# Stacks of queries and keys loaded by 5 DMAs with a repeated source in place of 13

## The reference

```python
q, k, v = jnp.split(x @ Wi.T + bi, 3, axis=-1)      # each to [B, H=16, T, HD=8]
scores = jnp.einsum('bhqd,bhkd->bhqk', q, k) / math.sqrt(HD)
scores = scores + mask[None]                        # causal, with ALiBi slopes
attn = jax.nn.softmax(scores, axis=-1)
out = jnp.einsum('bhqk,bhkd->bhqd', attn, v)
```

## Time and profile before

| | |
|---|---|
| median of 3 runs | 3465.85 us (3462.48 to 3480.17) |
| the profiled execution, its time | 3471.59 us |
| its span | 3469.4 us |
| PE busy | 2722.4 us (78%) |
| DVE busy | 1924.7 us (55%) |
| ACT busy | 1436.0 us (41%) |
| POOL busy | 478.3 us (14%) |
| DMA queue of SP | 95.62 MB, 12.6% of 16 engines' span |

### The profile page before, as it was taken

The page is one execution under the profiler, slowest core; times in us unless marked ns, Lnnn a source line. Parts: engine busy times, 40 slices in busy tenths (PEclk is TensorE's granted clock), DMA queues, the critical chain, the costliest instruction groups (busy, mean ns, idle before and its releaser), DMA issues. The chain is left out here.

```text
span 3469.4 us, 38736 instructions
## 1 busy us (share of the span) xinstructions
PE 2722.4 (78%) x12937; PEld 1118.8 (32%) x12937; DVE 1924.7 (55%) x3965; ACT 1436.0 (41%) x2856; POOL 478.3 (14%) x388
## 2 busy tenths in 40 slices
PE   6799876998869988699887689795266679599857
PEld 3233332332413333233343234342022234133225
DVE  4677236772357723677235562436899833677343
ACT  3266332663426643266434303234233243166510
POOL 1000010000100000100005500000688700100000
PEclk8699986999859998699987899897588889699977
DMA  3221012210132100321000000000000001312010
GB/s 82 47 42 30 13 45 48 44 31 13 29 64 45 31 13 14 79 41 34 13 17 1 6 1 0 22 1 12 0 0 0 0 24 36 80 31 44 14 74 13
DMA packets 57180, 98.20 MB, mean 28 GB/s; under 512 B 14438, under 2 KB 30310, under 8 KB 54502
## 3 DMA queue, kind: packets, MB, share of 16 engines
q1 hardware_dynamic: 56972, 95.62, 12.6%
HBM read 77.80 MB, written 16.78 MB: 27 GB/s over the span
## 5 line engine op out<-in xcount | busy, mean ns | idle before, releaser
L619 DVE CUSTOM_DVE_ANT_0 sb_masked_scores<-ps,sb_mask_row 128x128 f32<-128x128 f32 (+7 forms) x1280 | 912.7, 755 | 381.8 <-PE ps L548 375.1
L669 ACT ACTIVATE sb_prob<-ps 128x512 f32<-128x512 f32 (+3 forms) x1920 | 824.0, 495 | 428.5 <-PE ps L566 310.7
L548 PE MATMUL ps<-sb_k_stack,sb_q_stack 78*128 78x512 bf16 (+3 forms) x1920 | 555.8, 366 | 211.7 <-DMA sb_q_stack<-alibi 107.9
L563 PE MATMUL ps<-sb_q_stack,sb_k_stack 81*128 81x512 bf16 (+3 forms) x1920 | 573.4, 339 | 19.3 <-ACT sb_prob L669 2.6
L580 PE MATMUL ps<-sb_prob,sb_v_and_one 128*9 128x512 f32 (+3 forms) x3840 | 407.2, 498 | 2.1 <-ACT sb_o_raw L649 2.1
L563 PEld LDWEIGHTS ps<-sb_q_stack,sb_k_stack 81*128 81x128 bf16 x1920 | 184.2, 99 | 466.9 <-ACT sb_prob L669 311.1
L548 PEld LDWEIGHTS ps<-sb_k_stack,sb_q_stack 78*128 78x128 bf16 x1920 | 164.5, 102 | 445.6 <-DVE sb_row_max L619 230.0
L566 PE MATMUL ps<-sb_mask_kq,sb_ident_bf 128*128 128x128 bf16 x1280 | 267.6, 226 | 0.0
L1827 POOL TENSOR_TENSOR sb_inflow<-sb_delta_u,sb_b_spread 128x1024 f32<-128x1024 f32 x64 | 233.3, 3669 | 45.6 <-ACT sb_b_spread L1810 45.5
L1837 DVE TENSOR_TENSOR_SCAN sb_states<-sb_decay,sb_inflow 128x1024 f32<-128x1024 f32 x64 | 211.4, 3305 | 10.8 <-ACT sb_decay L1816 9.6
L258 ACT ACTIVATE sb_ln_squares<-sb_ln_centred 128x512 f32<-128x512 f32 x68 | 42.8, 629 | 373.9 <-DVE sb_ln_centred L224 373.8
(11 more groups left out here) (353 smaller groups left out, 3518.5 us busy)
## 6 DMA issues: line engine op xcount, KB each, us to landing
sb_k_stack<-k_parts SPq DMA_DIRECT2D x360, 64.0 KB
sb_q_stack<-q_parts SPq DMA_DIRECT2D x120, 192.0 KB
q_parts<-sb_qk_parts SPq DMA_DIRECT2D x80, 96.0 KB, 1.9
k_parts<-sb_qk_parts SPq DMA_DIRECT2D x80, 96.0 KB, 2.0
sb_unpick_sums<-unpick_sums SPq DMA_DIRECT2D x5, 1024.0 KB, 4.9
sb_l_weights<-l_weights SPq DMA_DIRECT2D x4, 1030.0 KB, 5.5
sb_l_gate_and_value<-l_up SPq DMA_DIRECT2D x1, 4096.0 KB, 12.8
sb_xpos<-xpos SPq DMA_DIRECT2D x1, 2048.0 KB
```

What stands on the lines that cost most here:

```text
L548: mm = pe.matmul(M.ps[:, bank + lo // CH, 0:hi - lo], A.qst[0:S1_ROWS, s, j, i * P:(i + 1) * P], A.kst[0:S1_ROWS, s, j, lo:hi], start=True ...
L563: mm = pe.matmul(out[:, a:CH], A.kst[0:S2_ROWS, s, j, kb * P:(kb + 1) * P], A.qst[0:S2_ROWS, s, j, half * CH + a:(half + 1) * CH], start=T ...
L619: dve.tensor_tensor_reduce(out=junk[:, done % 2, 0:w], in0=M.ps[:, bank:bank + 2, :].rearrange("p a q -> p (a q)")[:, 0:w], in1=M.mask_row ...
L669: act.activation(prob[:, st % PROB_STEPS, j, a:CH], M.ps[:, S2_BANK + v % S2_BANKS, a:CH], ACT.Exp).then_inc(exp_done, 1)
```

## The change

The queries' 72 rows are now written by one DMA. Its source is the 96 rows of the group in HBM, each of 1024 tokens, with a leading dimension of size 3 and step 0, so that the same rows are read three times. The keys' rows of one part (24 rows) are likewise written by one DMA, whose source is 32 rows of HBM repeated three times. That makes 3 DMAs for the keys, 1 for the queries and 1 for the bias. Nothing else differs: the same bytes land in the same places, and the waits and their order are as before.

```diff
-STACK_DMAS = 13
+STACK_DMAS = 5
...
 def load_q_stack(eng, A, q_aux, b, g, s, sem):
 
     tok = slice(b * T, (b + 1) * T)
+    rows = A.q_dram[g, :, tok]
+    eng.dma_start(A.qst[0:PAIR_ROWS, s, :, :],
+                  rows.unsqueeze(0).to_broadcast([3, 3 * DH * GROUP, T])).then_inc(sem, 16)
+    eng.dma_start(A.qst[PAIR_ROWS:S1_ROWS, s, :, :], q_aux[g]).then_inc(sem, 16)
+
+
+def load_k_stack(eng, A, b, g, s, sem):
+
+    tok = slice(b * T, (b + 1) * T)
     for k_part in range(3):
         at = 3 * DH * k_part
-        eng.dma_start(A.qst[at:at + 3 * DH, s, :, :],
-                      A.q_dram[g, :, tok].rearrange("(sd j) t -> sd j t", j=GROUP)).then_inc(sem, 16)
-    eng.dma_start(A.qst[PAIR_ROWS:S1_ROWS, s, :, :], q_aux[g]).then_inc(sem, 16)
-
-
-def load_k_stack(eng, A, b, g, s, sem):
-
-    tok = slice(b * T, (b + 1) * T)
-    for k_part in range(3):
-        part = A.k_dram[g, 4 * DH * k_part:4 * DH * (k_part + 1), tok].rearrange("(d j) t -> d j t", j=GROUP)
-        for q_part in range(3):
-            at = (3 * k_part + q_part) * DH
-            eng.dma_start(A.kst[at:at + DH, s, :, :], part).then_inc(sem, 16)
+        rows = A.k_dram[g, 4 * DH * k_part:4 * DH * (k_part + 1), tok]
+        eng.dma_start(A.kst[at:at + 3 * DH, s, :, :],
+                      rows.unsqueeze(0).to_broadcast([3, DH * GROUP, T])).then_inc(sem, 16)
```

More of the change, by code:

```diff
@@ L297, in load_q_stack @@
     tok = slice(b * T, (b + 1) * T)
-    for k_part in range(3):
-        at = 3 * DH * k_part
-        eng.dma_start(A.qst[at:at + 3 * DH, s, :, :],
-                      A.q_dram[g, :, tok].rearrange("(sd j) t -> sd j t", j=GROUP)).then_inc(sem, 16)
+    rows = A.q_dram[g, :, tok]
+    eng.dma_start(A.qst[0:PAIR_ROWS, s, :, :],
+                  rows.unsqueeze(0).to_broadcast([3, 3 * DH * GROUP, T])).then_inc(sem, 16)
     eng.dma_start(A.qst[PAIR_ROWS:S1_ROWS, s, :, :], q_aux[g]).then_inc(sem, 16)
@@ L308, in load_k_stack @@
     for k_part in range(3):
-        part = A.k_dram[g, 4 * DH * k_part:4 * DH * (k_part + 1), tok].rearrange("(d j) t -> d j t", j=GROUP)
-        for q_part in range(3):
-            at = (3 * k_part + q_part) * DH
-            eng.dma_start(A.kst[at:at + DH, s, :, :], part).then_inc(sem, 16)
+        at = 3 * DH * k_part
+        rows = A.k_dram[g, 4 * DH * k_part:4 * DH * (k_part + 1), tok]
+        eng.dma_start(A.kst[at:at + 3 * DH, s, :, :],
+                      rows.unsqueeze(0).to_broadcast([3, DH * GROUP, T])).then_inc(sem, 16)
 def qkv(nc, M, A, W, cols, scale, tables=None):
```

## The result

The changed kernel takes 3560.64 us (median of 4 runs, 3543.14 to 3566.77), the kernel before, run beside it, 3473.01 us. The ratio is 1.0247, with a 95% interval of 1.0213 to 1.0282: slower by 2.5%, some 88 us. Forecast were 63 us more, 3529 us, within 3475 to 3721. The profiled execution took 3561.09 us with a span of 3558.9 us, 89.5 us longer than the span before.

The account below looks back on a forecast made before the run. PE was taken to wait for stack loads at call starts, with loads between groups hidden until their deadline. Starts 24, maxima 9 and between groups 30 us sum to 63 us: 3529 us on the median, range 3475 to 3721.

Parts of the forecast that it names:

- Three engines: Stack loads: the source's outermost size 3 confines each DMA to three engines, busy share near 0.19, some 69 GB/s.
- One load: A stack's load, from first issue to PE: 20.0 us, of which 17.1 us at 69 GB/s.
- The starts: Start of each call: PE begins 4.8 us later, 24 us over five calls.
- Issue: SP's queue: fewer DMAs save about 5.5 us of issuing a load, worth nothing between groups.
- The copies of the maxima: Group 0 of each call: copies queue behind stacks 1 and 2, first `second` 1.8 us late, 9 us in all.
- Between groups: Loads inside calls: 20.0 us against a deadline of 18.37, 1.2 us lost per load, 30 us over five calls.
- Elsewhere: Outside the starts, the copies of the maxima and the loads between groups: the forecast's sum had no term.
- Spread over 12 engines: Rival for stack loads: DMAs spread by destination rows, loads of 11.2 to 11.8 us, about 3447 us; chance 0.08.
- Hidden between groups: Rival: three engines near 26.5 GB/s, loads in time between groups, +13 us at the starts, 3479 us; chance 0.10.
- Much slower for the pace of the engines: Rival for stack loads: three engines at only 14 to 18 GB/s each, 3721 to 3961 us; chance 0.22 (under 19).

Follow-up runs that it names:

- the version with other dimensions outermost: Five DMAs with 8 KB pieces, changed to 24 rows outermost for queries, 8 for keys without repeat, rows reordered: 3438.49 us, 0.9914 to the kernel before.
- FIRST_AHEAD 8: The changed kernel with FIRST_AHEAD, how far `first` runs ahead, at 8 in place of 10: 3492.29 us, 1.0059 to the kernel before.
- 8 KB pieces: The changed kernel's five DMAs, parts stored in HBM by sequence so a row's four heads form one 8 KB piece: 3497.62 us, 1.0098 to the kernel before.
- the queries alone: The kernel before with only the queries' three DMAs made one with a repeated source, the keys by nine as before: 3509.44 us, ratio 1.0133.

## Why the prediction was right, and where its sum was off

*Three engines.* Right: a busy share of 0.18 to 0.22 during loads, and 0.73 to 0.82 in the version with other dimensions outermost. The Trainium skill's rule on a leading zero-stride broadcast (DMA: Bandwidth & Descriptors, Rules for kernel authors) holds here for 3 copies. Its remedy is to put a dimension outermost whose size is a multiple of 16; the run with 24 and 8 outermost, 11.8 us a load, points the same way, but no load of a stack had a multiple of 16 there.

*One load, 20.0 us.* Measured 19.1 to 20.0. The pace was 69 to 81 GB/s for an assumed 69; the packets came a little later, at 1.6 to 2 us for 1.3.

*The starts, 24 us.* Measured 22.6. *Issue, 5.5 us less SP time, worth nothing:* right between groups; where the engines stay, five DMAs have a start 2.5 us shorter than 13.

*The copies of the maxima, 9 us.* Measured 0. The copies did stand behind stacks 1 and 2, as forecast, and in the first call the last landed 5.7 us after its issue. But a pace of some 75 GB/s, for 69, drained these stacks 51.5 us into the first call, for a forecast 53.5, and the last copy came 0.2 to 1.1 us ahead of its need. With FIRST_AHEAD 8, where the copies are wanted earlier, they were late by up to 1.4 us. The mechanism is there, its margin was mis-sized.

*Between groups, 30 us.* This term was mis-sized: 82 us. The waits were nearly as forecast, 25 us in 25 loads, 1.0 us each on average. What the sum left out is what comes behind them: 4 us of idle gaps and 53 us of granted clock at 0.50. The prediction named the clock at its end as what would make the loss larger, and priced it at nothing.

*Elsewhere, 0.* The profiled executions differ by 15.5 us in favour of the changed kernel outside the calls; in the stretch shown above it goes with the granted clock. 22.6 + 0 + 82.4 - 15.5 = 89.5 us. So the forecast of 63 came near partly by luck: two things that it didn't have, +57 and -15, and one that it had too much, 9, partly cancel. The time lies in the range because the range was stretched upwards for slower engines, and they were not slower.

*The rivals.* Spread over 12 engines, 3447 us: not what this change does, but near what its sibling does, with 3438 us; 11.8 us a load is as priced, though there the keys had 8 outermost and the pieces were longer. Hidden between groups, 3479: near it are the runs with FIRST_AHEAD 8 (3492) and with 8 KB pieces (3498). Much slower for the pace of the engines: no, three engines in this pattern run at some 24 GB/s each, the nine of the keys' loads before at 9. Pieces of 8 KB in the 13 DMAs changed nothing in the time (0.9992); why the crowded ones are so slow is open.

## What to carry to other kernels

Look at what stands outermost on both sides of a DMA before you merge small ones: the fewer DMAs here ran on 3 engines in place of 8 and 12. With pieces of 8 KB this cost 1.0%, and with other dimensions outermost the same count of DMAs gained 0.9%. Measure the slack of a prefetch from its issue to its use (18.4 us here, for a load of 15), since the loss rises steeply once it is used up: loads of 19.5 us cost 88 us, loads of 18.6 us cost 31. And price a stall of PE with the clock that it has afterwards: here 1 us of waiting cost 3.3 us on average. It cost 0.15 us over the wait itself where the clock kept 1.00, and 4.7 us over it where the clock stayed low for 10 us.

## What the runs showed of the hardware that was not expected

Waits of about a microsecond are enough for the granted clock to fall to 0.50, in 21 of 25 cases of the changed kernel, some 2 us behind the wait and for 3.4 or 10.2 us. The length of the wait alone doesn't tell whether it falls: in the changed kernel it fell behind waits of 0.60 to 1.46 us and kept 1.00 behind waits of 0.69 to 1.32 us, and with the queries alone it fell behind three waits of 0.52 to 0.80 us. Behind such a wait PE was not busy at once either: 1.64 of 3.00 us from 195 to 198. What decides is open.

SP's issue itself can stall. With three engines behind, the DMA of the bias kept SP for 4.5 to 7.9 us, against 0.47 before and 0.46 to 0.47 in the version with other dimensions outermost. No cost of it shows here: between groups the copies of the maxima, next in the queue, were issued only later.
